# Output projection and second normalisation joined to the attention block, in an adaLN attention and mixture-of-experts kernel

## The chip, the cores and the metric

The kernel runs on one core of one Trainium2 chip. The metric is the device time of one execution in microseconds. Before the change the median of three runs is 1806.25 us (1805.63 to 1806.42). All numbers of the profile come from one profiled execution.

## The reference

The input is x of shape (2, 2048, 256), float32. `mod` is silu(c) @ wmod, cut into shifts, scales and gates; the kernel computes:

```
h = layernorm(x) * (1 + ca) + sa
x = x + ga * (attention(h) @ W_o + b_o)      # 16 heads of 16, q also times W_s
h = layernorm(x) * (1 + cb) + sb             # "h2" in the kernel
scores = softmax(h @ router_w + router_b)    # 8 experts
G, idx = top_k(scores.T, 512)                # 512 tokens for each expert
x = x + gb * scatter_add(idx, G * (relu(h[idx] @ w1 + b1) @ w2 + b2))
```

The change lies in the lines from the output projection of attention to the choice of the top 512.

## The kernel before

The work runs as four blocks in a row. Each block gives every engine a program of its own, engines meet only at semaphores, and all engines (with what the block's own waits ask of the DMAs) meet at the end of a block.

**Block 1, L693 to L948, attention.** It starts with the projections of q, k and v. Then it goes through 64 units (16 heads x 2 batches x 2 halves of the queries). For each unit TensorE fills groups of scores for the row maxima (L220), which VectorE reduces (L227), makes the scores (L569), of which ScalarE takes the exponentials (L869), and weighs the values with them (L923). TensorE's order is written out by hand: in the loop at L933 block b first weighs block b-2, then makes scores of block b; two weighings stand behind the loop (L947). The last maxima are reduced one unit before the end. At the end of a unit ScalarE copies the output out (`take_output`, L851), SyncE stores it to DRAM and loads it back in another layout into `ao` (L744 to L764), with the sums of the softmax into `sums_c`. For every eight heads VectorE inverts the sums (`invert`, L877), SyncE spreads the inverses over the partitions (`load_inverse`, L719), and GpSimd multiplies `ao` by them (`normalise_part`, L807); each such part counts in the semaphore `normalised`.

**Block 2, L976 to L1146, the projection stage.** It runs over 8 chunks of 512 tokens. For each chunk n:
- TensorE `project(n)` (L1106, matmuls L1114): `ao` times the gated output matrix, in two halves of 8 matmul records, each into its own PSUM bank, once the residual add has emptied that bank;
- VectorE `body(n)` (L1042): adds each half to `xb` (L1047), takes mean and variance (L1053, L1058), waits for ScalarE's square root (L1022), refines 1/root (`newton`, L163), and writes the normalised rows `xn2` (L1067);
- TensorE `turn_h2` (L1098): transposes `xn2`; ScalarE `take_h2` (L1010) scales and shifts it into `h2_t`;
- TensorE `route` (L1123): the router's logits, which VectorE adds up (L1074);
- TensorE `turn_rows` (L1132): transposes h2 back to rows, ScalarE `take_rows` (L1017) copies them out, SyncE stores them to DRAM (L992) for the gathers of block 4.

TensorE's order is what matters here: it works on chunks n-2 and n at the same time. VectorE does the whole of body(n) before body(n+1):

```python
for n in range(chunks):                       # L1136
    if n > 1:
        turn_h2(n - 2, n % 2)
    project(n)
    if n > 1:
        route(n - 2, n % 2)
        turn_rows(n - 2, n % 2)
```

SyncE loads the weights of the first two experts at the start of block 2 (L982), stores each chunk of `xb` to the output (L990), and handles the last inverse (L987). GpSimd normalises the last two parts of `ao` there (L1002), which `project(4)` and `project(6)` wait for (L1108).

**Block 3, L1206 to L1358, the router.** Softmax over the logits, then a search for the 512th largest score of each expert, one bit per step: 30 probes. A probe is a count on VectorE (L1270), one matmul on TensorE (L1341, L1344) that adds the counts up, and a few VectorE instructions on single elements (L1280, L1283) that set the next candidate. VectorE and TensorE take turns; the other engines have next to nothing to do.

**Block 4, from L1383, the experts.** Lists of tokens, gathers, two layers of each of 8 experts, scatters.

Of the kernel before, what the change touches and what calls it, by code (L numbers as in the profile page):

```python
# [10 lines left out]
ALU = mybir.AluOpType  # L11
# [3 lines left out]
P = 128  # L15
NB = 2
# [13 lines left out]
E = 8  # L30
# [61 lines left out]
def adaln_moe_block(nc, x, w_q, b_q, w_k, b_k, w_v, b_v, w_o, b_o, w_s, router_w, router_b,  # L92
                    w1, b1, w2, b2, c, w_mod, out):
    ctx = ExitStack()
    with ctx:
# [596 lines left out]
        xb_in, xb_ready = [sem(f"xb_in{b}") for b in range(NB)], sem("xb_ready")  # L692
        with nc.Block() as block:  # L693
            pv_done, acc_out, v_staged = sem("pv_done"), sem("acc_out"), sem("v_staged")
# [5 lines left out]
            normalised = sem("normalised")  # L700
# [32 lines left out]
            def _(sp):  # L733
# [38 lines left out]
                for u in range(UNITS):  # L772
# [19 lines left out]
                load_output(UNITS - 1)  # L792

            @block.gpsimd
            def _(pool):
# [38 lines left out]
                for u in range(1, UNITS):  # L834
# [10 lines left out]
                    if u > 2 and done % HG == HG - 1:  # L845
                        normalise_part(done // HG, f)

            @block.scalar
            def _(act):
# [21 lines left out]
                take_output(UNITS - 1)  # L871

            @block.vector
            def _(dve):
# [13 lines left out]
                invert(UNITS - 2)  # L888

            @block.tensor  # L890
            def _(pe):
# [41 lines left out]
                for block in range(DELAY, blocks):  # L933
# [17 lines left out]
        h2_t = pt[:, 1:4:2, :].rearrange("p s (k t) -> p s k t", k=KD)  # L951
        ao_c = stage_a[:].rearrange("p s (t d) -> p s t d", d=D)
        xn2 = stage_b[:].rearrange("p s (t d) -> p s t d", d=D)
        h2_c = pt[:, 0:4:2, :].rearrange("p s (t d) -> p s t d", d=D)
        w_slots = v_all[:].rearrange("p t d -> p (t d)").rearrange("p (s n) -> p s n", s=2)
        w1_sb = [w_slots[:, s, 0:KD * FF].rearrange("p (k f) -> p k f", k=KD) for s in range(2)]
        w2_sb = [w_slots[:, s, KD * FF:].rearrange("p (f d) -> p f d", f=NF) for s in range(2)]
        w1_v = w1.rearrange("e (k p) f -> e p k f", p=P)
        w2_v = w2.rearrange("e (f p) d -> e p f d", p=P)
        w1_h = [kp[:, s, :].rearrange("p (k f) -> p k f", k=KD) for s in range(2)]  # L960
        weights_in = [sem(f"weights_in{s}") for s in range(2)]
        w1_high, w1_low = sem("w1_high"), sem("w1_low")

        def take_w1_high(act, e):
            act.wait_ge(weights_in[e % 2], e // 2 * 32 + 32)
            nc.scalar.copy(w1_h[e % 2], w1_sb[e % 2]).then_inc(w1_high, 1)

        out_stored = sem("out_stored")
        h2_stored = [sem(f"h2_stored{p}") for p in range(2)]
        h2_ready, xn2_ready, rows_turned = (sem(n) for n in ("h2_ready", "xn2_ready", "rows_turned"))  # L970
        y_full, y_out = sem("y_full"), sem("y_out")
        h2_turned, h2t_ready, l_full, l_out = sem("h2_turned"), sem("h2t_ready"), sem("l_full"), sem("l_out")
        var2_done, root2_done = sem("var2_done"), sem("root2_done")
        b_of = lambda n: slice(n // NCH, n // NCH + 1)

        with nc.Block() as block:  # L976
            @block.sync
            def _(sp):
                for par in range(2):
                    sp.sem_inc(h2_stored[par], 16)  # L980
                for e in range(2):
                    sp.dma_start(w1_sb[e], w1_v[e]).then_inc(weights_in[e], 16)  # L982
                    sp.dma_start(w2_sb[e], w2_v[e]).then_inc(weights_in[e], 16)
                for n in range(chunks):
                    if n == 2:
                        sp.wait_ge(normalised, G // HG * HALVES - 2)
                        load_inverse(sp, G // HG - 1, 1)  # L987
                    rows = slice(n * CT, (n + 1) * CT)
                    sp.wait_ge(y_out, n * 2 + 4)
                    sp.dma_start(out_rows[:, rows, :], xb[:, rows, :]).then_inc(out_stored, 16)  # L990
                    sp.wait_ge(h2_ready, n * 2 + 2)
                    sp.dma_start(h2_rows[:, rows, :], h2_c[:, n % 2]).then_inc(h2_stored[n % 2], 16)  # L992
                sp.wait_ge(out_stored, 16 * chunks)
                for par in range(2):
                    sp.wait_ge(h2_stored[par], 16 * pairs + 16)

            @block.gpsimd
            def _(pool):
                for f in range(HALVES):
                    pool.wait_ge(o_in[f], G * 32)  # L1000
                    pool.wait_ge(inverse_in[f], G * 16)
                    normalise(nc.gpsimd, G // HG - 1, f).then_inc(normalised, 1)  # L1002

            @block.scalar
            def _(act):
                def take_h2(n, par):
# [19 lines left out]
                for n in range(chunks):  # L1026
                    if n > 1:
                        take_h2(n - 2, n % 2)
                    root(n, n % 2)
                    if n > 1:  # L1030
                        take_rows(n - 2, n % 2)
# [600 lines left out]
```

## Time and profile before

| what | us |
|---|---|
| median of three runs | 1806.25 |
| the profiled execution | 1805.18 |
| its span (first to last instruction) | 1803.2 |
| block 1 ends on TensorE (last L923) | 1405.64 |
| block 2: first projection matmul (L1114) | 1412.48 |
| block 2: last logits (L1074) done | 1480.47 |
| block 3: first VectorE instruction (L1251) | 1486.47 |
| block 3: the 30 probes | 1492.47 to 1533.36 |
| block 4: first VectorE instruction (L1484) | 1542.92 |

All times but the first two are measured from the start of the span. In the rows, PE is TensorE (PEld its weight loads), DVE VectorE, ACT ScalarE, POOL GpSimd, SP SyncE; a "q" behind a name is the engine's queue. In a row of the timeline stand the start, the length, the engine, the line, the operation, output<-input and how many instructions were merged; in brackets the idle time before it and who ended it. A row of a table of windows gives the stretch, then busy time and instructions of each engine, the clock that TensorE was granted as a share of 2.4 GHz, the DMA share and GB/s. 0.50 of it is 1.2 GHz.

### The profile page before, as it was taken

How to read it: one execution, taken by the hardware profiler on the slowest of the kernel's cores; microseconds unless marked ns; L12 is line 12 of the kernel's file. 1: busy time of each engine (PE TensorE's matmuls, PEld its weight loads, DVE VectorE, ACT ScalarE, POOL GpSimd, SP SyncE). 2: the span in 40 equal slices, each digit the busy share in tenths (PEclk: the TensorE clock that was granted, in tenths of full speed). 3: DMA queues.
4: the chain of work that ended last, by engine and by line, in shares of the span. 5: the costliest groups of instructions: out<-in, count | busy, mean ns of one | idle time of the engine just before them, and what ended most of it. 6: DMA issues, size and time to landing. Idle time of an engine off the chain costs nothing. (4 is left out here: it accounts for less than half of the span.)

```text
span 1803.2 us, 42958 instructions
## 1 busy us (share of the span) xinstructions
PE 1692.5 (94%) x16862; PEld 951.5 (53%) x16862; DVE 1495.3 (83%) x1964; ACT 1215.3 (67%) x2304; POOL 245.8 (14%) x306
## 2 busy tenths in 40 slices
PE   7999999999999999999999999999999771599997
PEld 4645555555555555555555555555554670267886
DVE  5579999999999999999999999999995458645652
ACT  2327888888888888888888888888888330022231
POOL 0332013000000000000000000000000001235553
PEclk9999999999999999999999999999999885599999
DMA  7560442222233222223322222332200440025342
GB/s 253 189 180 28 101 97 39 38 41 38 52 64 52 38 40 40 38 52 63 51 41 39 41 37 52 61 53 41 39 14 14 145 164 0 24 74 137 83 128 24
DMA packets 93652, 121.95 MB, mean 68 GB/s; under 512 B 24060, under 2 KB 70716, under 8 KB 90348
## 3 DMA queue, kind: packets, MB, share of 16 engines
q1 hardware_dynamic: 84492, 109.22, 26.9%
q0 software_dynamic: 6144, 8.39, 2.7%
q8 instruction: 133, 2.18, 0.5%
q10 hardware_dynamic: 2816, 1.61, 0.3%
q14 instruction: 67, 0.55, 0.1%
HBM read 79.35 MB, written 38.54 MB: 65 GB/s over the span
## 5 line engine op out<-in xcount | busy, mean ns | idle before, releaser
L227 DVE TENSOR_REDUCE pmax<-ps 128x2 f32<-128x1024 f32 x1024 | 1192.6, 1216 | 53.2 <-PE ps L220 46.3
L869 ACT ACTIVATE pt<-ps 128x512 f32<-128x512 f32 x2048 | 1077.7, 599 | 181.4 <-PE ps L569 170.3
L220 PE MATMUL ps<-kp,qp 48*128 48x512 f32 x2048 | 626.5, 464 | 2.4 <-DVE pmax L227 2.4
L923 PE MATMUL ps<-pt,v_st 128*32 128x256 f32 (+1 forms) x10752 | 589.7, 335 | 0.2 <-ACT pt L869 0.2
L569 PE MATMUL ps<-qp,kp 50*128 50x512 f32 x2048 | 562.5, 422 | 0.5 <-ACT pt L869 0.5
L569 PEld LDWEIGHTS ps<-qp,kp 50*128 50x128 f32 x2048 | 294.4, 185 | 258.7 <-ACT pt L869 250.9
L923 PEld LDWEIGHTS ps<-pt,v_st 128*32 128x32 f32 x10752 | 265.7, 109 | 265.3 <-issue 192.3
L220 PEld LDWEIGHTS ps<-kp,qp 48*128 48x128 f32 x2048 | 246.1, 184 | 115.0 <-issue 90.0
L1452 ACT ACTIVATE ao<-ps,b_col 128x512 f32<-128x512 f32 x64 | 44.0, 688 | 156.5 <-PE ps L1591 156.5
L210 POOL CAST m_parts<-rowmax_t 128x32 fp32r<-128x32 f32 x64 | 13.4, 210 | 839.7 <-DVE rowmax_t L239 839.7
L1605 PE MATMUL ps<-v_all,ao 128*128 128x256 f32 x512 | 112.5, 381 | 0.8 <-ACT ao L1452 0.8
L1605 PEld LDWEIGHTS ps<-v_all,ao 128*128 128x128 f32 x512 | 96.7, 190 | 14.1 <-ACT ao L1452 1.2
L431 ACT ACTIVATE pt<-ps,xb 128x512 fp32r<-128x512 f32 x32 | 22.0, 687 | 61.3 <-PE ps L594 61.3
L1527 DVE TENSOR_TENSOR pt<-ps,b_row 128x256 f32<-128x256 f32 x32 | 13.5, 422 | 57.9 <-PE ps L1605 57.9
L594 PE MATMUL ps<-pt,xb 128*128 128x512 f32 x128 | 59.1, 603 | 1.7 <-ACT pt L415 1.7
L1420 POOL DMA_INDIRECT y<-pt,scatter_at x32 | 54.8, 1711 | 33.3 <-DVE pt L1531 24.9
L798 POOL COPY v_st<-v_all 128x256 f32<-128x256 f32 x32 | 12.6, 397 | 293.3 <-PE ps L923 293.3
L1490 DVE TENSOR_TENSOR stage_b<-lane,col_row 128x1024 bf16<-128x1024 int32 x32 | 37.7, 1222 | 13.4 <-PE ps L1564 13.1
L1444 ACT COPY list_t<-ps 128x128 f32<-128x128 f32 x8 | 2.1, 259 | 67.0 <-PE ps L1564 67.0
L1402 POOL DMA_INDIRECT stage_a<-h_rows,gather_at x32 | 33.0, 1032 | 84.5 <-DVE gather_at L1501 54.3
L1591 PE MATMUL ps<-qp,kp 128*128 128x512 f32 x96 | 40.0, 416 | 0.0
L1114 PE MATMUL ps<-wog,ao 128*128 128x256 f32 x128 | 33.3, 422 | 6.8 <-DVEq L1040 6.8
(196 smaller groups left out, 944.0 us busy)
## 6 DMA issues: line engine op xcount, KB each, us to landing
kp<-k_parts SPq DMA_DIRECT2D x186, 128.0 KB, 4.5
v_all<-L_ffn_w SPq DMA_DIRECT2D x16, 1024.0 KB, 8.4
qp<-q_parts SPq DMA_DIRECT2D x186, 64.0 KB, 4.0
q_parts<-pt SPq DMA_DIRECT2D x16, 512.0 KB, 2.7
k_parts<-pt SPq DMA_DIRECT2D x16, 512.0 KB, 3.0
o_rows<-o_sb SPq DMA_DIRECT2D x64, 128.0 KB, 2.0
sums_c<-o_rows SPq DMA_DIRECT2D x512, 0.5 KB
m_rows<-m_parts SPq DMA_DIRECT2D x256, 2.0 KB
```

The source lines that it names most:

```text
L220: last = nc.tensor.matmul(slot[:, half * CH:(half + 1) * CH], qp[rows, r, a * P:(a + 1) * P], kp[rows, r, c * CH:(c + 1) * CH], start=True ...
L227: v.reduce_max(pmax[:, u % 2, 2 * k:2 * k + 2], slot.rearrange("p (f t) -> p f t", f=2), AX.X).then_inc(groups_out, 1)
L569: nc.tensor.matmul(bank(n % SCORE_BANKS), kp[rows, h % NBUF, kt * P:(kt + 1) * P], qp[rows, h % NBUF, f * CH:(f + 1) * CH], start=True, st ...
L594: last = mm(unit_bank(n, u), w[:, k, (u % 2) * P:(u % 2 + 1) * P], h_t[n % 2][:, k, :], start=k == 0, stop=k == KD - 1)
L869: nc.scalar.activation(pt[:, s % PTS, half * CH:(half + 1) * CH], bank(n % SCORE_BANKS), ACT.Exp, scale=SCALE).then_inc(scores_out, 1)
L923: last = mm(acc[32 * j:32 * (j + 1), first * QB:(first + many) * QB], v_st[:, h % NBUF, kt, :], probs[:, :, j * QB:(j + 1) * QB], start=kt ...
L1114: last = mm(bank(2 + half)[:, t * D:(t + 1) * D], ao[:, n // NCH * KD + k, at:at + P], wog[:, n // NCH, k, :], start=k == 0, stop=k == KD - 1)
L1420: nc.gpsimd.indirect_dma_start(out_flat, bass.IndirectOffsetOnAxis(ap=scatter_at[:, par, cc:cc + 1], axis=0), contrib[:, cc, :], None, com ...
L1452: nc.scalar.activation(hid[:, f, :], bank(2 + f % 2), ACT.Relu, bias=b1_col[:, bass.ds(e * NF + f, 1)]).then_inc(hid_out, 1)
L1490: v.tensor_tensor(one_hot[:, g8 % 2], lane[:, bass.ds(n, 1), g8 * 8:(g8 + 1) * 8].squeeze(1).unsqueeze(2).broadcast_to([P, 8, P]), col_row ...
L1591: last = mm(bank(2 + f % 2), w[:, k, f * P:(f + 1) * P], t[:, k, :], start=i == 0, stop=i == len(products) - 1)
L1605: last = mm(bank(eo_banks[cc])[:, 0:D], hid[:, f, cc * P:(cc + 1) * P], w2_sb[par][:, f, :], start=f == 0, stop=f == NF - 1)
```

## The change

Block 2 is gone; its work is spread over blocks 1 and 3.

- Block 1 goes on into the projection stage with no meeting of the engines in between. `project_rows(0)` is issued by TensorE after the scores of the last block but one of attention; all others come after the last weighing, in the new order `project_rows(1)`, then for each n `turn_h2(n)`, `project_rows(n + 2)`, `route(n)`.
- VectorE does residual and variance of chunk n+1 first and then normalises the rows of chunk n. The inversion of the last sums is placed between them: `invert_first` behind residual(0), `invert_last` ahead of residual(3).
- ScalarE takes the square root of chunk n+1 ahead of `take_h2(n)`; the last attention output is taken behind root(0). h2 is written into `ao` in place of `h2_t`.
- SyncE issues the four weight loads in unit 62 of attention.
- `turn_rows`, the copies of the rows and the stores of h2 go to block 3: in half chunks of 4 transposes, two ahead of the router's own transposes and one behind every second probe. Their ScalarE copies and the SyncE stores are in block 3 too. TensorE's loop over the probes is written out.

The diff, cut to its core (banks and semaphores renamed with it are left out):

```diff
+        def post_act(act, take_last_output):
+            root(0)
+            take_last_output()
+            act.wait_ge(late_out, 1)
+            for n in range(chunks):
+                if n + 1 < chunks:
+                    root(n + 1)
+                take_h2(n)
...
+            def residual(n):
+                par = n % 2
+                for half in range(2):
+                    dve.wait_ge(y_full, n * 2 + half + 1)
+                    rows = xb[:, n * CT + half * 2:n * CT + half * 2 + 2, :]
+                    v.tensor_tensor(rows, y_bank(half).rearrange("p (t d) -> p t d", d=D), rows, ALU.add).then_inc(y_out, 1)
+                dve.wait_ge(y_out, n * 2 + 2)
+                for t in range(CT):
+                    last = v.bn_stats(stats[:, par, t, :], xb[:, n * CT + t, :])
...
+            def normalise_rows(n):
+                par = n % 2
+                at = slice(par * CT, (par + 1) * CT)
+                dve.wait_ge(root2_done, n + 1)
+                newton(v, link, rstd2[:, par, :], nwt[:, 0, at], nwt[:, 1, at], nwt[:, 2, at])
+                if n > 1:
+                    dve.wait_ge(h2_turned, n - 1)
+                for t in range(CT):
+                    last = v.tensor_scalar(xn2[:, par, t, :], xb[:, n * CT + t, :], mv[:, par * CT + t, 0:1],
+                                           rstd2[:, par, t:t + 1], ALU.subtract, ALU.mult)
+                last.then_inc(xn2_ready, 1)
...
+            dve.wait_ge(xb_ready, 2 * NB)
+            dve.wait_ge(late_in, 16 * 6)
+            residual(0)
+            invert_first()
+            for n in range(chunks):
+                if n + 1 == 3:
+                    invert_last()
+                if n + 1 < chunks:
+                    residual(n + 1)
+                normalise_rows(n)
+                if n > 0:
+                    take_logits(n - 1)
+            take_logits(chunks - 1)
+
+        def project_rows(pe, n):
...
+            for half in range(2):
+                if n > 0:
+                    pe.wait_ge(y_out, n * 2 + half - 1)
...
+        def post_pe(pe):
+            def turn_h2(n):
+                pe.wait_ge(xn2_ready, n + 1)
+                if n > 0:
+                    pe.wait_ge(h2t_ready, n * 2)
...
+            project_rows(pe, 1)
+            for n in range(chunks):
+                turn_h2(n)
+                if n + 2 < chunks:
+                    project_rows(pe, n + 2)
+                route(n)
+
...
+                    if u == UNITS - 2:
+                        sp.wait_ge(v_staged, G)
+                        for e in range(2):
+                            sp.dma_start(w1_sb[e], w1_v[e]).then_inc(weights_in[e], 16)
+                            sp.dma_start(w2_sb[e], w2_v[e]).then_inc(weights_in[e], 16)
...
+                    if block == blocks - DELAY:
+                        project_rows(pe, 0)
                 for block in range(blocks - DELAY, blocks):
                     weigh(block)
...
+                post_pe(pe)
...
-                for n in range(chunks):
-                    if n > 1:
-                        turn_h2(n - 2, n % 2)
-                    project(n)
-                    if n > 1:
-                        route(n - 2, n % 2)
-                        turn_rows(n - 2, n % 2)
...
+                    for g in range(2 * chunks):
+                        n, half = divmod(g, 2)
+                        act.wait_ge(rows_turned, g + 1)
+                        if n > 1 and half == 0:
+                            act.wait_ge(h2_stored[n % 2], n // 2 * 16)
+                        nc.scalar.copy(h2_c[:, n % 2, half * 2:half * 2 + 2, :],
+                                       bank(6 + half).rearrange("p (t d) -> p t d", d=D)).then_inc(h2_ready, 1)
...
+                    turn_rows(0)
+                    turn_rows(1)
                     pe.wait_ge(score_done, 1)
...
-                    for j in range((TOPBIT + 1) // (BITS + 1) * (BITS + 1), TOPBIT + 1):
+                    for j in range(TOPBIT + 1):
                         pe.wait_ge(counted, j + 1)
                         mm(bank(1)[:, 0:1], same[:], count[:], start=True, stop=True).then_inc(totalled, 1)
+                        if j % 2 and j // 2 + 2 < 2 * chunks:
+                            turn_rows(j // 2 + 2)
```

## Rows read from the trace of the kernel before

**Rows 1.** Section 2 of the page: granted clock of TensorE in 40 slices, in tenths.

```profile
PEclk9999999999999999999999999999999885599999
```

**Rows 2.** Windows by block: end of block 1, block 2, block 3.

```profile
1378.00:1405.70 27.70, 27.45 (x309) 13.32 (x308) 0.55 (x1) 23.83 (x48) 0.09 (x1) 1.00 0.12 33
...
1412.50:1480.50 68.00, 62.19 (x378) 56.60 (x379) 44.98 (x169) 20.21 (x39) 4.28 (x2) 0.90 0.54 187
...
1486.40:1542.90 56.50, 8.15 (x41) 4.07 (x41) 45.29 (x235) 1.70 (x2) 10.00 (x24) 0.50 0.00 0
```

**Rows 3.** Timeline, the end of attention and the start of block 2.

```profile
1404.78 0.86 PE L923 MATMUL ps<-pt,v_st 128*32 128x128 f32 x16 [0.19 <-ACT pt L869]
...
1412.48 10.19 PE L1114 MATMUL ps<-wog,ao 128*128 128x256 f32 x32 [6.84 <-DVEq L1040]
...
1416.35 0.69 DVE L1047 TENSOR_TENSOR xb<-ps,xb 128x512 f32<-128x512 f32 x1 [21.66 <-PE ps L1114]
1419.26 0.69 DVE L1047 TENSOR_TENSOR xb<-ps,xb 128x512 f32<-128x512 f32 x1 [2.22 <-PE ps L1114]
```

**Rows 4.** Timeline, one later chunk of block 2 at full clock.

```profile
1447.39 1.04 PE L1098 MATMUL ps<-ident,stage_b 128*128 128x128 f32 x8
...
1448.27 3.62 PE L1114 MATMUL ps<-wog,ao 128*128 128x256 f32 x16
...
1451.72 1.85 PE L1123 MATMUL ps<-rw_sb,pt 128*128 128x8 f32 x16
1451.92 0.69 DVE L1047 TENSOR_TENSOR xb<-ps,xb 128x512 f32<-128x512 f32 x1 [0.72 <-PE ps L1114]
...
1454.20 0.19 DVE L1074 TENSOR_TENSOR logits<-ps,rb_row 128x32 f32<-128x32 f32 x1
...
1454.33 1.04 PE L1098 MATMUL ps<-ident,stage_b 128*128 128x128 f32 x8
...
1455.15 0.18 DVE L165 RECIPROCAL rstd<-nwt 128x4 f32<-128x4 f32 x1 [0.27 <-ACT nwt L1022]
...
1456.15 1.39 DVE L1067 TENSOR_SCALAR stage_b<-xb,mv,rstd 128x256 f32<-128x256 f32 x4
```

**Rows 5.** Windows of 2 us in block 2, at its start and around two idle times of TensorE.

```profile
1416.00:1418.00 2.00, 2.00 (x6) 1.62 (x5) 0.69 (x1) 0.00 (x0) 0.00 (x0) 0.50 1.04 382
1422.00:1424.00 2.00, 0.68 (x4) 0.24 (x2) 1.55 (x8) 0.20 (x1) 0.00 (x0) 1.00 1.00 302
1426.00:1428.00 2.00, 2.00 (x7) 1.62 (x6) 1.81 (x9) 0.00 (x0) 0.00 (x0) 0.50 0.31 108
1470.00:1472.00 2.00, 0.64 (x6) 0.64 (x6) 1.38 (x4) 1.31 (x2) 0.00 (x0) 1.00 0.59 209
1474.00:1476.00 2.00, 2.00 (x11) 2.00 (x10) 0.00 (x0) 0.92 (x2) 0.00 (x0) 0.50 0.04 8
```

**Rows 6.** Timeline, TensorE behind the first of the idle times.

```profile
1424.84 1.40 PE L1098 MATMUL ps<-ident,stage_b 128*128 128x128 f32 x8 [2.16 <-DVE stage_b L1067]
...
1426.03 5.03 PE L1114 MATMUL ps<-wog,ao 128*128 128x256 f32 x16
```

**Rows 7.** Timeline, the end of block 2.

```profile
1471.36 1.95 PE L1123 MATMUL ps<-rw_sb,pt 128*128 128x8 f32 x16 [2.11 <-ACT pt L1010]
...
1474.83 1.91 PE L1098 MATMUL ps<-ident,stage_b 128*128 128x128 f32 x8
...
1480.28 0.19 DVE L1074 TENSOR_TENSOR logits<-ps,rb_row 128x32 f32<-128x32 f32 x1 [6.73 <-PE ps L1123]
```

**Rows 8.** Timeline, the matmul of a probe on TensorE.

```profile
1519.26 0.19 PE L1341 MATMUL ps<-count,same 128*128 128x1 bf16 x1 [1.09 <-DVE above L1270]
```

**Rows 9.** Timeline, the inversion of the sums of unit 62.

```profile
1394.14 0.55 DVE L717 RECIPROCAL sums_c<-sums_c 128x64 f32<-128x64 f32 x1 [16.65 <-DMA sums_c<-o_rows]
```

**Rows 10.** Timeline, GpSimd normalises the last part of ao.

```profile
1450.78 2.35 POOL L730 TENSOR_TENSOR ao<-ao,stage_a 128x1024 f32<-128x1024 f32 x1 [36.35 <-DMA stage_a<-inverse_sums]
```

**Rows 11.** Timeline, VectorE's first instruction of block 4.

```profile
1542.92 0.29 DVE L1484 TENSOR_TENSOR in_quarter<-quarter,codes 128x128 bf16<-128x128 int32 x1 [1.02 <-PEq L1573]
```

More of the change, by code:

```diff
@@ L692, in adaln_moe_block @@
         xb_in, xb_ready = [sem(f"xb_in{b}") for b in range(NB)], sem("xb_ready")
+        acc_out, normalised = sem("acc_out"), sem("normalised")
+        ao_c = stage_a[:].rearrange("p s (t d) -> p s t d", d=D)
+        xn2 = stage_b[:].rearrange("p s (t d) -> p s t d", d=D)
+        h2_c = pt[:, 0:4:2, :].rearrange("p s (t d) -> p s t d", d=D)
+        w_slots = v_all[:].rearrange("p t d -> p (t d)").rearrange("p (s n) -> p s n", s=2)
+        w1_sb = [w_slots[:, s, 0:KD * FF].rearrange("p (k f) -> p k f", k=KD) for s in range(2)]
@@ new lines, in project_rows @@
+        def project_rows(pe, n):
+            if n == 0:
+                pe.wait_ge(xb_ready, 2 * NB)
+                pe.wait_ge(groups_out, STEPS)
+                pe.wait_ge(normalised, G // HG // NB * HALVES)
+            if n >= NCH and n % 2 == 0:
+                pe.wait_ge(normalised, (G // HG - 1) * HALVES + (n - NCH) // 2 + 1)
+            for half in range(2):
+                if n > 0:
+                    pe.wait_ge(y_out, n * 2 + half - 1)
+                for t in range(2):
+                    at = (n % NCH) * CH + (half * 2 + t) * P
+                    for k in range(KD):
+                        last = nc.tensor.matmul(y_bank(half)[:, t * D:(t + 1) * D], ao[:, n // NCH * KD + k, at:at + P],
+                                                wog[:, n // NCH, k, :], start=k == 0, stop=k == KD - 1)
+                last.then_inc(y_full, 1)
@@ L846, in _ @@
                         normalise_part(done // HG, f)
+                for f in range(HALVES):
+                    normalise_part(G // HG - 1, f)
             @block.scalar
@@ L956, in adaln_moe_block @@
[L956 to L972, printed above, removed]
@@ L1206, in adaln_moe_block, with _ @@
             with nc.Block() as block:
+                @block.sync
+                def _(sp):
+                    for n in range(chunks):
+                        sp.wait_ge(h2_ready, n * 2 + 2)
+                        sp.dma_start(h2_rows[:, n * CT:(n + 1) * CT, :], h2_c[:, n % 2]).then_inc(h2_stored[n % 2], 16)
+                    for par in range(2):
+                        sp.wait_ge(h2_stored[par], 16 * pairs)
                 @block.gpsimd
@@ L1332, in _, with turn_rows @@
                     mm = nc.tensor.matmul
+                    def turn_rows(g):
+                        n, half = divmod(g, 2)
+                        if g > 1:
+                            pe.wait_ge(h2_ready, g - 1)
+                        for t in range(2):
+                            for k in range(KD):
+                                at = (half * 2 + t) * P
+                                last = nc.tensor.transpose(bank(6 + half)[:, t * D + k * P:t * D + (k + 1) * P],
+                                                           h2_of(n)[:, k, at:at + P], ident[:])
+                        last.then_inc(rows_turned, 1)
+                    turn_rows(0)
+                    turn_rows(1)
                     pe.wait_ge(score_done, 1)
```

237 lines of the change are left out of this document (80 added, 157 removed).

## The prediction

> **What bounds the kernel now.** I read the slices of the page first, then a table of windows by block, then the timeline around the two seams, then the clock in windows of 2 us. In the slices TensorE's clock leaves 2.4 GHz only in slices 32 to 35 of 40 [rows 1], and that is where the change works; the rest is attention and experts, which keep their work. The windows show three different limits. At the end of attention TensorE is busy 27.45 of 27.7 us [rows 2]. Then it is idle for 6.84 us while the last output is stored and the engines meet [rows 3]. Block 2 lasts 68 us with TensorE busy 62.2 of them and VectorE only 45.0. In the router VectorE is busy 45.3 of 56.5 us and TensorE 8.2, at a granted clock of 0.50 [rows 2]. So before, block 2 is TensorE's, and the change goes for that: it takes the seam away and moves TensorE work (`turn_rows`) to where TensorE idles.
>
> One steady chunk of block 2 has a period of 1454.33 - 1447.39 = 6.94 us: the turn, the projection, the logits and the turn of the rows follow each other without a hole, and VectorE waits 0.72 us for the second half of y [rows 4]. It can be so short because `project(n)` stands behind `turn_h2(n-2)`: while VectorE normalises chunk n-1, its next y is already being made.
>
> **The new chain.** In the new order `project_rows(n+2)` stands behind `turn_h2(n)`, which waits for xn2(n). VectorE makes xn2(n) at the end of its loop n, after residual(n+1), and its next piece of work is residual(n+2), which needs just the y that TensorE has not begun. So nothing overlaps there: xn2(n), turn, projection, residual, statistics, normalising, xn2(n+1) is a chain of one chunk's length. Its price from one chunk [rows 4]:
> - xn2 done to first transpose: 0.06, an estimate from the 0.03 between the end of the projection (1448.27 + 3.62) and the add at 1451.92;
> - first transpose to first projection matmul: 1448.27 - 1447.39 = 0.88;
> - first projection matmul to VectorE's second add: 1451.92 - 1448.27 = 3.65 (the first half's add is hidden beside the second half's matmuls);
> - second add to the end of xn2: 1456.15 + 1.39 - 1451.92 = 5.62, less some 0.1 for the logits add, which now stands behind, and 0.25 for the wait for the root, which now has a residual's time to come: 5.25.
>
> Sum 9.84 us at full clock against 6.94 before. TensorE's own work in it is 0.88 + 3.45 + 1.85 = 6.2, so it idles 3.6 us per chunk.
>
> **The clock.** Before, two idle times of TensorE, 2.16 us ahead of 1424.84 [rows 6] and 2.11 us ahead of 1471.36 [rows 7], were each followed by a fall of the granted clock from 1.00 to 0.50, the lower of its two levels, 1.2 GHz [rows 5]. The new idle time is 3.6 us in every chunk, longer than both, so I take the fall in every chunk. What it costs: 8 transposes take 1.91 instead of 1.04 [rows 4, 7], up to 0.87. The projection of a chunk took 5.03 where the clock came back soon [rows 6] and 1419.26 - 1412.48 = 6.78 where it came back late [rows 3], against 3.65: 1.4 to 3.1. Together 1.4 to 4.0 per chunk; I take 2.3, since the turn in front uses up a part of the slow stretch before the projection starts. The cycle is then 12.15 us.
>
> **The sum**, against the profiled execution (1805.18 us; the median of the three runs is 1.07 more).
> - Attention: 16 matmul records of chunk 0 go in ahead of the last but two weighing. TensorE is the busy engine there [rows 2], so I take their whole 1451.72 - 1448.27 = 3.45 us, bounds 0 (ScalarE's queue of scores covers it) and 3.65. Attention then ends at 1404.78 + 0.86 + 3.45 = 1409.1 [rows 3, 4].
> - y of chunk 1 directly behind, at full clock: 1409.1 + 3.65 = 1412.7, and xn2(0) at + 5.25 = 1417.9. (ScalarE's table load falls between the last exponential and the first root: 0.)
> - Six cycles until xn2(6): 6 x 12.15 = 72.9, to 1490.8.
> - The last two chunks have no projection to hide behind. Turn, ScalarE, matmuls and add of the logits of one chunk took 1480.47 - 1474.83 = 5.64 [rows 7]. Two of them in a row, as TensorE's order has it (turn 7 stands behind route 6), are 0.06 + 5.64 + 5.45 = 11.1: 1501.9.
> - To the router: 1.0 us, as between blocks 3 and 4 [rows 11]. Before, it was 6.0 (1480.47 to 1486.47), because the last rows of h2 had still to be copied and stored; that 5 us is a true gain. Router starts at 1502.9 instead of 1486.47: +16.4.
> - Probes: 14 of 30 get four transposes behind their matmul. TensorE idles 1.09 us there [rows 8]. At the low clock eight transposes took 1.91 us [rows 7], so four take 0.96 and fit: 0. That halving forgets what a burst pays once, the first load and the last drain; if these are most of the difference between 1.04 and 1.91 and the next matmul has to wait for them, four take up to 0.96 + 0.3 and each pair of probes grows by up to 0.2, 2.6 in all (below nothing it can't go, TensorE only gets work). I take 0, since the burst as a whole is the nearest row. Loop or no loop on TensorE changes nothing; it waits for VectorE.
> - ScalarE's 16 copies and SyncE's 8 stores in the router lie beside the probes and end some 8 us ahead of the block, where these two engines have nothing else [rows 2]: 0. No gain either.
> - The four weight loads, 1 MB each, now issue near 1384. At the 382 GB/s at which they ran before [rows 5] the 4.2 MB take about 11 us, so the store of unit 62 behind them on SyncE's queue is late by up to those 11 us, and its sums come near 1402 to 1405 instead of 1394.1 [rows 9]. VectorE asks for them only after residual(0): chunk 0's projection ends some 4 us ahead of 1409, and a residual takes 3 of the 5.25 us, so near 1408: hidden. Part 1 of `ao` was normalised by 1450.78 + 2.35 = 1453.1, its inverse asked for behind the rows of chunk 1 [rows 10]; that point stays near 1430, so it is ready by about 1453 again, and `project_rows(6)` wants it near 1467. Part 0 is asked for 20 us before part 1 and wanted near 1443. Both hidden, with 14 us or more to spare.
>
> 1805.18 + 16.4 = 1821.6; as a median **1822 us**. Its own range: the clock's bounds move six cycles by -5.4 to +10.2, the ends seldom in all of them, the insertion -3.4, the probes +2.6: about 1815 to 1830.
>
> **A rule weighed.** The chain rests on TensorE not taking `project_rows(n+2)` ahead of the waiting turn. The Trainium skill, "TensorE: Matmul & The Clock Gate", in "Step-by-step: what each phase is for", says that only weight loads are pulled ahead and matmuls stay in program order; no row here shows a matmul that passed a waiting one, so the trace agrees as far as it goes. The same page, in Part 1, advises to count the warm-up as under 1% of a kernel; by that the clock's share would be anything under 18 us; mine is 6 x 2.3 + 1.7 = 15.5, near that bound, from rows.
>
> **Rivals.**
> - *Faster, the gain as meant.* If VectorE's and TensorE's work did overlap, the cycle would be the larger of TensorE's 6.2 and VectorE's 6.94 - 0.72 = 6.2 [rows 4]. xn2(6) would come at 1417.9 + 37.3 = 1455.2. The last two chunks at full clock take 11.1 less twice 0.87, 9.4, and 1.0 to the router: 1465.6, -20.9, **1785 us**. For it speaks the slack of two chunks before; against it that no y(n+2) can exist before xn2(n) in the new order. Chance 0.07.
> - *Same, the clock holds.* The chain is as I say, but TensorE stays at 2.4 GHz: xn2(6) at 1417.9 + 6 x 9.84 = 1476.9, end 1476.9 + 9.4 + 1.0 = 1487.3, +0.8: **1807 us**. For it: over half of each cycle is work. Against it: both falls came after shorter gaps [rows 5 to 7]. Chance 0.07. It decides at an idle time that the clock survives; if it does so in about half of the chunks, 1811 to 1815, chance 0.08.
> - *Slower still, the clock never comes back.* At the low clock half a chunk took 3.87 (1412.48 to 1416.35) [rows 3], a whole one 7.3; the cycle is 0.06 + 1.9 + 7.3 + 5.25 = 14.5, six of them 87, the end at +30: **1836 us**. Against it: before, it came back within the 10.19 us of the first two chunks [rows 3], as the window at 1422 shows [rows 5], and the new burst is longer. Chance 0.05.
> - *It doesn't do what it says.* Chunk 0 could wait inside attention for the normalised parts and stall it; but four parts are long there by then, and y's banks are free since the last maxima, one unit earlier. The place of chunk 0 is worth 3.5 us either way. Within my range.
>
> **How the numbers follow.** Forecast 0.73 (1815 to 1830), the rivals 0.07, 0.07, 0.08 and 0.05. The range 1811 to 1830 leaves out the first, second and fourth. A measurement of this kernel can tell about 0.2% (3.6 us) from no change: faster 0.07, same 0.08, slower 0.85.
>
> **What would show it.** Right: VectorE idles about 5 us per chunk ahead of the adds, released by TensorE's projection; xn2 to xn2 takes 11.5 to 12.6 us; the granted clock in the stage averages near 0.7; router starts near 1503 and its 30 probes last the same 41 us as before. Wrong: a period near 6.3 (no chain), near 9.8 (clock holds), probes with transposes 0.2 us longer than the others, or a wait of a projection on GpSimd's normalised parts.

## The result and the profile after

The changed kernel takes 1825.37 us (median of four runs, 1823.73 to 1826.92) against 1806.34 for the kernel before on the same chip (1805.63 to 1806.68): a ratio of 1.0109, 95% interval 1.0093 to 1.0125. It is slower by 19 us; forecast were 1822.0, in a range of 1811 to 1830. Its profiled execution took 1825.83 us, with a span of 1823.7.

Where the 20.65 us between the two profiled executions lie, by the first VectorE instruction of each part:

| part | before | after | difference |
|---|---|---|---|
| last weighing of attention ends | 1405.64 | 1409.00 | +3.36 |
| router begins | 1486.47 | 1507.77 | +21.30 |
| router, length | 56.45 | 55.58 | -0.87 |
| experts, to the end of the span | 260.28 | 260.35 | +0.07 |

In the page's slices of the granted clock (tenths of full speed), slices 32 and 33 have fallen from 8 to 7 [rows 1]:

```profile
PEclk9999999999999999999999999999999775599999
```

Windows of the kernel after: the whole joined stage behind attention, its steady part from the first turn to the seventh xn2, its tail, and the router. Columns are as in [rows 2].

```profile
1409.00:1507.40 98.40, 65.51 (x304) 58.20 (x304) 45.51 (x158) 13.88 (x26) 4.67 (x2) 0.74 0.17 57
1419.90:1493.30 73.40, 51.02 (x240) 45.37 (x240) 35.43 (x128) 9.92 (x18) 2.34 (x1) 0.78 0.19 65
1493.30:1507.40 14.10, 10.81 (x48) 9.92 (x48) 2.53 (x12) 2.90 (x4) 0.00 (x0) 0.51 0.00 0
...
1507.70:1563.30 55.60, 23.45 (x105) 14.58 (x105) 45.32 (x235) 10.87 (x18) 10.02 (x24) 0.50 0.21 76
```

In the steady part both engines idle: TensorE is busy 51.0 and VectorE 35.4 of 73.4 us. Before, TensorE was busy 62.2 of 68 [rows 2]. Two engines that wait for each other show just this: both are well under the stretch, and their sum, 86.4, lies only 13 us above it, 2.2 for each of the six chunks. So they hardly work at the same time: only the logits lie beside VectorE's work, and the first add beside the second half of the projection. The router has the same VectorE time as before, 45.3 us.

One cycle of the chain on the timeline of the kernel after (to be read against [rows 4]):

```profile
1431.70 0.41 DVE L787 TENSOR_SCALAR stage_b<-xb,mv,rstd 128x256 f32<-128x256 f32 x1
...
1432.16 1.97 PE L835 MATMUL ps<-ident,stage_b 128*128 128x128 f32 x8 [3.45 <-DVE stage_b L787]
...
1433.92 4.39 PE L824 MATMUL ps<-wog,ao 128*128 128x256 f32 x16
...
1436.62 0.69 DVE L768 TENSOR_TENSOR xb<-ps,xb 128x512 f32<-128x512 f32 x1 [3.96 <-PE ps L824]
...
1438.15 1.85 PE L846 MATMUL ps<-rw_sb,ao 128*128 128x8 f32 x16
1438.35 0.69 DVE L768 TENSOR_TENSOR xb<-ps,xb 128x512 f32<-128x512 f32 x1 [1.04 <-PE ps L824]
```

TensorE waits 3.45 us for xn2 (L787), turns, projects; VectorE waits 3.96 and 1.04 us for the two halves of y. Each names the other in its brackets. The turn takes 1.97 us where it took 1.04, and the logits at the end of the same burst take the 1.85 of full clock. So the clock falls and comes back inside each cycle, as windows of 2 us of the same stretch show in the last but two of their columns:

```profile
1430.00:1432.00 2.00, 0.00 (x0) 0.00 (x0) 1.86 (x8) 0.06 (x1) 0.00 (x0) 1.00 0.00 0
1432.00:1434.00 2.00, 1.84 (x9) 1.84 (x10) 0.67 (x3) 0.00 (x0) 0.00 (x0) 0.52 0.07 16
1434.00:1436.00 2.00, 2.00 (x8) 1.65 (x8) 0.00 (x0) 1.45 (x2) 0.00 (x0) 0.63 0.27 72
1436.00:1438.00 2.00, 2.00 (x11) 1.77 (x10) 0.69 (x1) 0.00 (x0) 0.00 (x0) 1.00 0.37 100
```

### The profile page after: what moved, and what is told of

The parts are those of the page before. It is cut to its first block and busy times, and to the rows that moved or that the text cites. A ratio compares the mean times of both kernels' runs of the same rounds, so it can differ in the third digit from the quotient of the medians.

```text
span 1823.7 us, 42883 instructions
## 1 busy us (share of the span) xinstructions
PE 1712.3 (94%) x16862; PEld 965.0 (53%) x16862; DVE 1499.2 (82%) x1964; ACT 1217.4 (67%) x2304; POOL 245.5 (13%) x306
## 5 line engine op out<-in xcount | busy, mean ns | idle before, releaser
L227 DVE TENSOR_REDUCE pmax<-ps 128x2 f32<-128x1024 f32 x1024 | 1192.6, 1216 | 53.1 <-PE ps L220 46.2
L1619 PEld LDWEIGHTS ps<-v_all,ao 128*128 128x128 f32 x512 | 96.7, 190 | 14.2 <-ACT ao L1466 1.2
L768 DVE TENSOR_TENSOR xb<-ps,xb 128x512 f32<-128x512 f32 x16 | 11.1, 692 | 67.3 <-PE ps L824 67.3
L972 POOL COPY v_st<-v_all 128x256 f32<-128x256 f32 x32 | 12.6, 397 | 293.2 <-PE ps L1104 293.2
L835 PE MATMUL ps<-ident,stage_b 128*128 128x128 f32 x64 | 15.4, 420 | 29.6 <-DVE stage_b L787 29.6
```

Source lines behind the costliest of these rows:

```text
L227: v.reduce_max(pmax[:, u % 2, 2 * k:2 * k + 2], slot.rearrange("p (f t) -> p f t", f=2), AX.X).then_inc(groups_out, 1)
L1619: last = mm(bank(eo_banks[cc])[:, 0:D], hid[:, f, cc * P:(cc + 1) * P], w2_sb[par][:, f, :], start=f == 0, stop=f == NF - 1)
```

## The experiments

All are edits of the kernel after, but one, which is said. Each ratio is to runs of the kernel before that were made beside it, and in brackets stands its 95% interval. Positions are from single profiled executions. In these attention ran its own length, give or take 1 us, but for two: its last maximum (L227) starts between 1374.7 and 1375.6 in most, at 1377.7 in the one with TensorE's order, and at 1378.3 in the first one with chunk 0 behind attention. Where it matters, positions are counted from there. The theory: the order makes a chain through two engines, and the clock adds to it. The rivals are that something else that came with the change does the harm (the place of chunk 0, GpSimd, the rows in the router), or the clock alone.

### VectorE's order: the chain broken on VectorE's side

```diff
             for n in range(chunks):
+                normalise_rows(n)
                 if n + 1 == 3:
                     invert_last()
                 if n + 1 < chunks:
                     residual(n + 1)
-                normalise_rows(n)
```

> VectorE normalises the rows of chunk n ahead of the residual of chunk n+1; nothing else differs from the changed kernel. Chain theory (the order made turn, projection, residual and normalising one serial chain): the y that VectorE wants next is already made, the cycle falls from 12.2 us to 6.2 to 6.9, TensorE has no idle time above 1 us in the stage and keeps 2.4 GHz. First rows near 1412, last near 1457, router near 1464 instead of 1507.8: some 44 us less, 1780 to 1786 us, faster than both kernels. Rival (the stage is slow because of the seam's removal or of work on ao, not of the order): the cycle stays above 9 us and the time above 1810.

Measured: **1784.15 us**, 0.9886 [0.9870, 0.9903]. The one moved line turns +19 us into -20. The timeline of this kernel, from one xn2 to the next:

```profile
1423.57 1.38 DVE L787 TENSOR_SCALAR stage_b<-xb,mv,rstd 128x256 f32<-128x256 f32 x4
...
1425.16 1.85 PE L846 MATMUL ps<-rw_sb,ao 128*128 128x8 f32 x16
1425.33 1.22 DVE L768 TENSOR_TENSOR xb<-ps,xb 128x512 f32<-128x512 f32 x2
...
1426.86 1.07 PE L835 MATMUL ps<-ident,stage_b 128*128 128x128 f32 x8
...
1427.77 3.40 PE L824 MATMUL ps<-wog,ao 128*128 128x256 f32 x15
...
1429.89 1.38 DVE L787 TENSOR_SCALAR stage_b<-xb,mv,rstd 128x256 f32<-128x256 f32 x4
```

No brackets stand behind these rows: neither engine waits for the other. VectorE's two adds run as one, since y(n+1) lies ready when it has written xn2(n). The period is 1429.89 - 1423.57 = 6.32 us, 5.92 in four of the other chunks and 7.80 in the first, against 12.24 on average in the kernel after. That is the engines' own work: in a window of 24 us TensorE is busy all the time and VectorE 22.2 us, where the kernel after has 15.4 and 13.3, at a clock of 1.00 where it has 0.78. These are the windows from 1424 to 1448, first of the kernel after, then of this one:

```profile
1424.00:1448.00 24.00, 15.39 (x78) 13.94 (x78) 13.28 (x43) 2.69 (x6) 2.34 (x1) 0.78 0.22 68
```

```profile
1424.00:1448.00 24.00, 24.00 (x161) 22.37 (x160) 22.21 (x84) 5.80 (x12) 2.36 (x1) 1.00 0.40 133
```

The clock came back with no edit to it; it was low only from 1420 to 1424 (0.58 and 0.57), where a projection took 5.30 us behind the longer first period, and in the tail. So the chain is the cause, and the low clock in the steady part its consequence.

### TensorE's order: the chain broken on TensorE's side

```diff
             for n in range(chunks):
-                turn_h2(n)
                 if n + 2 < chunks:
                     project_rows(pe, n + 2)
+                turn_h2(n)
                 route(n)
```

> TensorE projects chunk n+2 ahead of the turn of chunk n; VectorE as in the changed kernel. Chain theory: y(n+2) is made while VectorE takes statistics and normalises, so the chain breaks here too, but TensorE now waits 1.5 us for ScalarE between turn and logits: cycle about 0.9 + 1.5 + 1.9 + 3.4 = 7.7 us, router near 1478, 1794 to 1800 us. Rival (only VectorE's order matters): no gain, 1825.

Measured: 1806.01 us, 1.0005 [0.9995, 1.0014]. The chain's length is gone in part, but both expectations missed, the one by 6 to 12 us, the other by 19. The timeline of this kernel:

```profile
1442.13 1.04 PE L835 MATMUL ps<-ident,stage_b 128*128 128x128 f32 x8
...
1444.71 1.95 PE L846 MATMUL ps<-rw_sb,ao 128*128 128x8 f32 x16 [1.54 <-ACT ao L744]
...
1446.51 5.39 PE L824 MATMUL ps<-wog,ao 128*128 128x256 f32 x16
1449.88 0.69 DVE L768 TENSOR_TENSOR xb<-ps,xb 128x512 f32<-128x512 f32 x1 [2.41 <-PE ps L824]
```

With the projection ahead of the turn nothing stands between the turn and the logits, so TensorE waits 1.54 us for ScalarE's scaling in every chunk. The clock falls in some of the chunks (0.78 from 1424 to 1448), the projection takes 5.39 us instead of 3.6, and VectorE waits again. From one xn2 to the next, in order, it is 5.6, 13.6, 6.2, 9.6, 9.6 and 7.9 us, 8.8 on average; in the 13.6 lie a projection of 6.27 us at the low clock and a VectorE instruction that GpSimd held up for 1.7 us (more of that below). The projection between turn and logits does two jobs: it makes the next y, and it fills the time that ScalarE needs. So TensorE's order in the change has a use, and the order to change is VectorE's.

### The clock alone

Dummy matmuls into bank 0 keep TensorE busy while it would wait.

```diff
+            def warm(many):
+                for i in range(many):
+                    nc.tensor.matmul(bank(0)[:, 0:D], ident[:], wog[:, 0, 0, :], start=True, stop=True)
+
             project_rows(pe, 1)
+            warm(14)
             for n in range(chunks):
                 turn_h2(n)
                 if n + 2 < chunks:
                     project_rows(pe, n + 2)
+                else:
+                    warm(3)
                 route(n)
+                if n + 2 < chunks:
+                    warm(7)
```

> The changed kernel with matmuls whose result nobody reads, in a bank of its own, in TensorE's idle times of the projection stage: 14 behind chunk 1, 7 behind the logits of each chunk, 3 between turn and logits of the last two. The order, and with it the chain, stays. Clock theory: the granted clock stays 1.00, the cycle goes from 12.24 to 9.84 us (6 x 2.4 = 14), and the tail loses two slow turns and two slow passes of the logits (3.58 against 1.85 us, 1.97 against 1.04), some 5 us: 1805 to 1810 us. Rival (the clock costs little, the chain nearly all): 1820 or more.

Measured: 1808.40 us, 1.0021 [1.0011, 1.0030]. One cycle of this kernel:

```profile
1450.53 1.38 DVE L787 TENSOR_SCALAR stage_b<-xb,mv,rstd 128x256 f32<-128x256 f32 x4
1451.97 1.09 PE L835 MATMUL ps<-ident,stage_b 128*128 128x128 f32 x8 [0.33 <-DVE stage_b L787]
1452.90 3.62 PE L824 MATMUL ps<-wog,ao 128*128 128x256 f32 x16
...
1460.21 1.38 DVE L787 TENSOR_SCALAR stage_b<-xb,mv,rstd 128x256 f32<-128x256 f32 x4
```

Its length is 1460.21 - 1450.53 = 9.68 us: the chain at full clock, which the prediction had put at 9.84. Four of the six cycles take 9.68 or 9.69. The second takes 11.72, since GpSimd held a VectorE instruction for 2 us in it, and the third 11.36: behind that hold TensorE waited 2.36 us in spite of the dummy matmuls, and its clock fell once. The window shows it:

```profile
1442.00:1444.00 2.00, 2.00 (x6) 1.56 (x5) 0.00 (x0) 1.34 (x2) 0.00 (x0) 0.50 0.00 0
```

It fell once more in the tail. So "full clock" holds for most of this run, not for all of it, and the expectation that it stays at 1.00 was missed there. The run is nearly the rival *the clock holds* (1807 us). By the ratios the clock is worth (1.0109 - 1.0021) x 1805 = 16 us of the kernel after, and between 11 and 21 by the ends of their intervals. The other 24 us down to VectorE's order are mostly waiting at full clock.

### GpSimd

The kernel after has two places where an instruction on a handful of elements takes as long as a GpSimd instruction beside it. The timeline:

```profile
1415.44 2.34 POOL L893 TENSOR_TENSOR ao<-ao,stage_a 128x1024 f32<-128x1024 f32 x1 [37.63 <-DMA stage_a<-inverse_sums]
...
1415.55 2.25 DVE L166 TENSOR_TENSOR nwt<-rstd 128x4 f32<-128x4 f32 x1
...
1440.45 2.34 POOL L893 TENSOR_TENSOR ao<-ao,stage_a 128x1024 f32<-128x1024 f32 x1 [22.67 <-DMA stage_a<-inverse_sums]
1440.52 0.38 DVE L774 BATCH_NORM_AGGREGATE mv<-stats 128x2 f32<-128x6 f32 x4
1440.93 1.88 DVE L777 TENSOR_SCALAR nwt<-mv 128x4 f32<-128x4 f32 x1
```

L166 ends 0.02 us behind GpSimd's instruction (1417.80 and 1417.78), L777 0.02 too (1442.81 and 1442.79); their like take 0.16 and 0.17. They lie on the chain, so 2.1 and 1.7 us go straight onto it. The experiment lets GpSimd begin each part only when an xn2 is ready, that is, while VectorE waits for y:

```diff
                 for f in range(HALVES):
+                    pool.wait_ge(xn2_ready, (1, 3)[f])
                     normalise_part(G // HG - 1, f)
```

> The changed kernel, but GpSimd multiplies the last two parts of ao only once the rows of chunk 0 and of chunk 2 are normalised, that is in VectorE's idle time. Theory (a small VectorE instruction on SBUF can't go on while GpSimd's 2.3 us multiplication runs): the two VectorE instructions of 2.25 and 1.88 us fall back to 0.16 and 0.17, and the time by 3 to 4 us, to about 1821.5. Rival (they were long for another reason, such as waiting for a semaphore inside): they stay, and so does the time, 1825.

Measured: 1822.31 us, 1.0099 [1.0083, 1.0116]; the interval overlaps that of the kernel after, so the times alone don't show the 3 us. The timeline does:

```profile
1415.25 0.16 DVE L166 TENSOR_TENSOR nwt<-rstd 128x4 f32<-128x4 f32 x1
...
1416.05 1.38 DVE L787 TENSOR_SCALAR stage_b<-xb,mv,rstd 128x256 f32<-128x256 f32 x4
...
1417.51 2.35 POOL L893 TENSOR_TENSOR ao<-ao,stage_a 128x1024 f32<-128x1024 f32 x1 [39.99 <-DVE stage_b L787]
```

xn2(0) is done at 1417.4 instead of 1419.8, and no short instruction is held. It is a real cost and a small one: it was not the cause of the 19 us.

### The place of chunk 0

```diff
-                    if block == blocks - DELAY:
-                        project_rows(pe, 0)
...
+                project_rows(pe, 0)
                 post_pe(pe)
```

> The changed kernel with chunk 0 projected behind the last weighing instead of inside attention. Chain theory: attention ends 3.4 us earlier and chunk 0 takes the same 3.5 us behind it, so the rows of chunk 0 (which wait for the residual of chunk 1) are ready at the same time, and the stage after it is the same chain: within 1 us of the changed kernel, 1825 to 1826. Rival (beginning inside attention brings the projection forward by a chunk): 3 to 4 us slower, 1829.

Measured: 1822.98 us, 1.0096 [1.0079, 1.0113], no slower than the kernel after, and 2 us under what was expected; the rival's 1829 is out. Counted from the last maximum, the last weighing ends after 1408.16 - 1378.3 = 29.9 us, in the kernel after 1409.00 - 1375.5 = 33.5: the insertion does cost attention its 3.6 us. But xn2(0) is done after 42.2 us here and after 42.2 us in the run with GpSimd held back, which has chunk 0 inside. In both kernels VectorE makes xn2(0) behind residual(1), so it waits for attention and both projections, in whatever order TensorE does these. The place of chunk 0 is worth nothing in this kernel, neither way. In the kernel after xn2(0) is done after 44.3 us, 2.1 more, which is the hold by GpSimd: here part 0 moved to 1422.03, out of the way of L166, which takes 0.16 us (the second hold stayed, 1.94 us on L777). The median is 2.4 us under that of the kernel after, about as much, but the intervals of the two ratios overlap. What the place is worth without the chain is tried below.

### The rows in the router, and the rows in block 2

To price the part of the change that moves work to the router, the rows were left out on both sides. The stores of h2 stay and write what stands in their buffer, so these two kernels gather other rows and give another output. In the kernel after, without `turn_rows` and its copies in the router:

```diff
-                    turn_rows(0)
-                    turn_rows(1)
...
-                        if j % 2 and j // 2 + 2 < 2 * chunks:
-                            turn_rows(j // 2 + 2)
```

> The changed kernel with the turning of the rows of h2 and their copies left out of the router (the stores of h2 then write whatever stands in their buffer, so the experts gather other rows). Theory (the transposes fit between two probes): the same 40.3 us for the probes, the same time as the changed kernel within 0.5 us, 1825. Rival (the transposes or the copies delay the probes): up to 2.6 us less, 1822.5.

Measured: 1825.21 us, 1.0112 [1.0095, 1.0129]. In the router they cost nothing. In the kernel before, without `turn_rows` and `take_rows` in block 2:

```diff
                     if n > 1:
                         route(n - 2, n % 2)
-                        turn_rows(n - 2, n % 2)
```

> The kernel before with the turning of the rows and their copies left out of the projection stage (the stores of h2 write what stands in their buffer). It is what moving them out would give at best in the old order, where nothing else is moved. Theory (block 2 is TensorE's): the cycle falls from 6.94 to about 6.3 us, where VectorE binds, some 4 to 5 us in eight chunks, and the end of the block comes 3 to 5 us earlier without the last turn, copy and store: 1795 to 1799 us. Rival (VectorE is the bound already): only the end, 1801 or more.

Measured: 1796.04 us, 0.9949 [0.9933, 0.9966]. There they cost 9.5 us of 1805.58: the period of this kernel is 1455.12 - 1448.99 = 6.13 us against 6.94 [rows 4], and the block closes 0.3 us behind the last logits instead of 6.0. So moving the rows is a gain by itself, and the chain took it. The timeline:

```profile
1448.99 1.07 PE L1094 MATMUL ps<-ident,stage_b 128*128 128x128 f32 x8
...
1455.12 1.07 PE L1094 MATMUL ps<-ident,stage_b 128*128 128x128 f32 x8
```

### A version that beats both

VectorE's order, GpSimd's parts held until the sixth and the eighth half of y have been added, the turn of chunk 7 ahead of the logits of chunk 6, and dummy matmuls in the two waits of the tail:

```diff
-            for n in range(chunks):
+            for n in range(chunks - 1):
                 turn_h2(n)
                 if n + 2 < chunks:
                     project_rows(pe, n + 2)
-                route(n)
+                    route(n)
+            warm(5)
+            turn_h2(chunks - 1)
+            route(chunks - 2)
+            warm(2)
+            route(chunks - 1)
...
+                    pool.wait_ge(y_out, (6, 8)[f])
```

> VectorE's order of the first experiment, and three edits at the rims of the stage: the turn of chunk 7 stands ahead of the logits of chunk 6, 5 and 2 matmuls that nobody reads keep TensorE busy in the two waits of the last chunks, and GpSimd starts its first multiplication only behind the residual adds of chunk 2. Theory (what is left behind the rows is slow for a low clock and for two chunks in series): the logits of the last chunks take 1.85 instead of 3.5 us and one wait for ScalarE is hidden, 5 to 7 us less than the 1784.2 of the first experiment, and 1 us for GpSimd: 1776 to 1779 us. Rival (the tail waits for the last rows of VectorE anyway): 1782 or more.

Measured: **1778.08 us**, 0.9855 [0.9839, 0.9872]: 27.5 us under the kernel before. One of its four runs took 1782.67, at a mean granted clock of 0.973 where the others have 0.976, so the dummy matmuls may not hold the clock every time. The tail of this kernel, beside that of the kernel after, shows what a low clock does to the logits. First the kernel after:

```profile
1496.71 3.58 PE L846 MATMUL ps<-rw_sb,ao 128*128 128x8 f32 x16 [1.54 <-ACT ao L744]
...
1503.63 3.58 PE L846 MATMUL ps<-rw_sb,ao 128*128 128x8 f32 x16 [1.54 <-ACT ao L744]
...
1507.77 0.25 DVE L1253 TENSOR_SCALAR same_i<-iota_i 128x128 int32<-128x128 int32 x1 [0.33 <-PEq L857]
```

Then this one:

```profile
1454.98 1.09 PE L835 MATMUL ps<-ident,stage_b 128*128 128x128 f32 x8 [1.68 <-DVE stage_b L787]
1455.90 1.85 PE L846 MATMUL ps<-rw_sb,ao 128*128 128x8 f32 x16
...
1458.56 1.85 PE L846 MATMUL ps<-rw_sb,ao 128*128 128x8 f32 x16
...
1460.96 0.25 DVE L1263 TENSOR_SCALAR same_i<-iota_i 128x128 int32<-128x128 int32 x1 [0.33 <-PEq L866]
```

The same without the seven dummy matmuls:

```diff
-            warm(5)
             turn_h2(chunks - 1)
             route(chunks - 2)
-            warm(2)
             route(chunks - 1)
```

> The kernel with VectorE's order and the edited tail (1778.1 us) without the 7 matmuls that nobody reads. Theory: TensorE then idles over 3 us ahead of the turn of chunk 7, the clock falls to 1.2 GHz, the turn takes 1.9 and both passes of the logits up to 3.6 instead of 1.85 us, of which one turn and about two passes are in the chain: 3 to 4 us slower, 1781 to 1782. Rival (the order of the turns made the gain of the edited tail): 1778 to 1779.

Measured: 1781.38 us, 0.9873 [0.9856, 0.9889]. TensorE waits 3.81 us ahead of the last turn, which then takes 1.97, and the two passes of logits take 6.83 together instead of 2 x 1.85. The router begins at 1464.00 against 1460.96; by the timeline seven matmuls that compute nothing are worth 3 us. What is left down from VectorE's order alone, 1784.15 to 1781.38, is at most GpSimd's place and the turn of chunk 7; they were not tried apart, and the intervals of the three ratios overlap. And with the dummy matmuls, but chunk 0 behind attention, by the edit shown above:

> The kernel with VectorE's order and the edited tail (1778.1 us), with chunk 0 projected behind attention. Here VectorE binds the stage, and its first rows wait only for chunk 0. Theory: attention ends 3.4 us earlier but VectorE's residual of chunk 0 ends 3 us later, and all behind it: 1780.5 to 1781.5 us, so beginning inside attention is worth 3 us in this order, though it was worth nothing in the serial one. Rival (TensorE's sum binds, which is the same either way): 1778.

Measured: 1784.48 us, 0.9889 [0.9873, 0.9906]: 6.4 us above the version that beats both, where about 3 were expected. The timeline of this kernel says why it is more than the y that comes later:

```profile
1414.68 1.45 PE L835 MATMUL ps<-ident,stage_b 128*128 128x128 f32 x8 [2.09 <-DVE stage_b L787]
...
1460.02 2.05 PE L852 MATMUL ps<-wog,ident 128*128 128x256 f32 x4
...
1461.86 3.42 PE L846 MATMUL ps<-rw_sb,ao 128*128 128x8 f32 x16
```

The first xn2 starts at 1413.24 instead of 1410.65, 2.6 later, and the last one at 1455.76 instead of 1453.54, 2.2 later. In the tail the clock fell in spite of the dummy matmuls, which cost another 2.7 by the router's start at 1465.84. Together 4.9; what is left of the 6.4 may lie between the two sets of runs, which was not tried. Where VectorE makes xn2(0) before residual(1), the place of chunk 0 is worth at least 2.2 us.

## Why the prediction was right, point by point

The direction and the mechanism held: the two orders make one chain of both engines. What was off were two terms of the sum (the tail and the closing) and one thing that wasn't in it (GpSimd's hold); in the profiled executions the router began 4.9 us later than forecast, 1507.77 against 1502.9. There is also a slip of the last step: 1821.6 and the 1.07 up to the median make 1822.7, not 1822.

- *Attention* ends at 1409.00, forecast 1409.1. The projection of chunk 0 costs its whole length there, as said. That its place is worth 3.5 us either way was wrong: in this kernel it is worth nothing, since xn2(0) needs y(1) too.
- *y(1), xn2(0).* The second add began at 1412.69 (forecast 1412.7). xn2(0) ended at 1419.81 instead of 1417.9: 1.9 late. This is the step that was missing. The prediction asked of GpSimd's parts only whether they come in time, and they did: part 0 was done at 1417.8, part 1 at 1442.8, each more than 20 us before its projection. It did not ask what GpSimd's instruction does to the engine beside it. The run with GpSimd held back ended xn2(0) at 1417.4.
- *The cycle at full clock*, 9.84 forecast, is 9.68 in the run with the clock kept up. *The clock's share*, 2.3 forecast, is 12.24 - 9.68 = 2.6, in which the second hold by GpSimd has 1.7 / 6 = 0.3: 2.3. *Six cycles* took 1493.27 - 1419.81 = 73.5 us against 72.9. The single ones take 12.30, 12.99, 11.61, 12.62, 11.37 and 12.57, inside and just beyond the 11.5 to 12.6 that was to be seen. Without the hold in the second, the clock costs 1.6 to 1.9 us in three of them and 2.6 to 2.9 in the other three; that 2.3, taken from the range 1.4 to 4.0, hit the mean is in part luck. VectorE's idle time of 5 us per chunk (3.96 + 1.04), its releaser and a clock near 0.7 (0.74) are as told.
- *The tail* is the mis-sized term: 14.2 us (1493.27 to 1507.44) against 11.1. The step took the last chunk of block 2, 5.64 us, for one at the low clock, since its turn of 1.91 us was [rows 7]. But its logits, 3.5 us later, were at full clock again, as a row and a window of the kernel before show that the prediction did not look at:

```profile
1478.28 1.96 PE L1123 MATMUL ps<-rw_sb,pt 128*128 128x8 f32 x16 [1.54 <-ACT pt L1010]
```

```profile
1478.00:1480.00 2.00, 1.72 (x16) 1.72 (x17) 0.00 (x0) 0.23 (x1) 0.00 (x0) 1.00 1.00 353
```

  In the kernel after the clock is 0.51 over the tail, and the same pass takes 3.58 us. Two passes with 1.6 us more each are 3.2, the miss. The full clock there goes with `turn_rows`, which filled TensorE between logits and turn: in the kernel before with the rows left out, the last two passes (1465.57 and 1472.49) take 3.58 us too.
- *The closing* took 0.33 us against 1.0; it goes the other way. The 0.33 of the row at 1507.77 is the meeting of the engines alone, with no DMA to wait for.
- Sum: 16.4 + 1.9 + 0.6 + 3.1 - 0.7 = 21.3, the measured shift.
- *Probes*: 0 forecast with a bound of 2.6. They last 40.3 us against 40.9, and leaving the rows out gains nothing. Four transposes take 1.10 us, between the 0.96 that was estimated and its bound. They fill TensorE's idle time and the next probe's matmul still comes 1.28 us after the one before. The timeline of the kernel after:

```profile
1548.14 0.19 PE L1356 MATMUL ps<-count,same 128*128 128x1 bf16 x1 [1.09 <-DVE above L1272]
1548.19 1.10 PE L1343 MATMUL ps<-ident,ao 128*128 128x128 f32 x4
...
1549.42 0.19 PE L1356 MATMUL ps<-count,same 128*128 128x1 bf16 x1
```

- *Weight loads, the sums of unit 62, copies and stores*: hidden, as said; the sums were inverted at 1407.89.
- *The rule weighed.* The clock's share by the ratios is 16 us, 0.9% of the time, and 0.6 to 1.1% with their intervals. The Trainium skill, "TensorE: Matmul & The Clock Gate", Part 1, puts the warm-up at under 1% of a typical kernel. The run agrees with that, though it can't exclude a little more.
- *The rivals.* The time of the gain as meant, 1785, is what the kernel with VectorE's order gives (1784.15): its price was right, its condition (that the engines overlap) is what the order of VectorE denied. The time of the held clock, 1807, is what the run with dummy matmuls gives (1808.40). Neither happened.

## What to carry to other kernels

When two engines hand the same chunk back and forth, write each one's order side by side and ask of every hand-over which other work its maker could have done first: here the projection of n+2 was begun only after xn2(n), and VectorE made xn2(n) last. One line moved on VectorE (first give what the other engine needs, then take what it gave) was worth 40 us of 1825. Remove a seam only after that, and keep the engine with the clock busy right to the end of the stage, since a pass of small matmuls at the low clock takes nearly twice as long.

## What the runs showed of the hardware that was not expected

- **GpSimd holds short VectorE instructions.** While its multiplication of 128x1024 elements ran (2.34 us), L166 took 2.25 us and L777 1.88 us, both to within 0.02 us of its end, where they take 0.16 and 0.17; the run with VectorE's order has 7.80 us from its first xn2 to its second, the version that beats both, with GpSimd held back, 6.14. The aggregation L774 ran beside it unharmed (0.38 us). It is not the same instruction each time: at the second part in the run with dummy matmuls it was L168 that took 2.21 us, while L167, begun 0.01 us ahead of GpSimd's, took 0.16. That agrees with the Trainium skill, "SBUF — State Buffer", section "Who interferes with whom": a VectorE instruction with two inputs in SBUF, or a `tensor_scalar` in a mode that takes two ports, has to wait for the end of a GpSimd instruction that reads SBUF and began before it. L166 has two such inputs (the same tile twice); that L777 and L168, both `tensor_scalar`, ran in such a mode was not shown.
- **The logits pass and the turn take nearly twice as long at the low clock.** The logits pass, 16 matmuls of 8 columns, takes 1.85 us when other work is in front and 1.95 alone at full clock, and 3.58 at the low one, a factor of 1.8 to 1.9; eight transposes take 1.04 to 1.09 and 1.97; a projection of 16 matmuls, into which the clock's return falls, 4.4 to 5.7 instead of 3.6.
- **The meeting of the engines costs 0.33 us** between two blocks when no DMA is waited for: from the last add of the logits (done at 1507.44) to VectorE's next instruction (1507.77). In the kernel before it was 6.0 us.
